# Fused convolution block and window-attention block: the order of a strip, the second MLP bias, and who subtracts the softmax maxima

## The reference, cut to what matters

```python
x = relu(bn3(conv1x1(relu(bn2(conv3x3_grouped(relu(bn1(conv1x1(x)))))))) + x)
shortcut = x
y = roll(layernorm(x, norm1_w, norm1_b), (-3, -3))      # then cut in 7x7 windows
q, k, v = y @ qkv_w.T
attn = softmax(q @ k.T * 0.25 + bias(cpb MLP) + mask)
x = shortcut + unroll((attn @ v) @ proj_w.T + proj_b)
z = layernorm(x, norm2_w, norm2_b)
return x + gelu(z @ fc1_w.T + fc1_b) @ fc2_w.T + fc2_b
```

## Time and profile before

| | |
|---|---|
| median of 3 runs | 4876.97 us (4873.29 to 4880.41) |
| the profiled execution, its own time | 4880.38 us |
| span of that execution in the profile | 4878.6 us |
| busy over the span: PE, DVE, ACT, POOL | 94%, 75%, 73%, 52% |
| granted TensorE clock, mean over the span | 0.99 of full speed |
| convolution stage | its last sums on DVE end about 754 us after the span's start |
| attention stage | the remaining 4120 us or so, 256 strips |

### The profile page before, as it was taken

One profiled execution on the slowest core, in us unless ns is written; L12 is line 12 of the kernel. 1 busy time (PEld: TensorE's weight loads), 2 busy tenths in 40 slices (PEclk: granted clock), 3 DMA queues, 4 the chain that ended last, 5 costly groups with the idle time before them and its releaser, 6 DMA issues.

```text
span 4878.6 us, 192818 instructions
## 1 busy us (share of the span) xinstructions
PE 4590.0 (94%) x71190; PEld 3230.5 (66%) x71190; DVE 3646.7 (75%) x7461; ACT 3537.4 (73%) x5899; POOL 2552.6 (52%) x3498
## 2 busy tenths in 40 slices
PE   8999996999999999999999999999999999999998
PEld 5666664666666666666666666666666666666665
DVE  4343435888888888888888888888888888888886
ACT  3344444778778777877877877877787787787786
POOL 4344433555555555555555555555555555555554
PEclk9999998999999999999999999999999999999999
DMA  4445441100000100100100000010010010000000
GB/s 134 153 145 158 144 136 39 28 26 27 26 26 26 28 26 26 28 27 26 28 27 26 27 28 27 26 28 26 26 28 27 26 28 27 27 27 26 26 26 24
DMA packets 298299, 218.70 MB, mean 45 GB/s; under 512 B 43247, under 2 KB 245486, under 8 KB 298158
## 3 DMA queue, kind: packets, MB, share of 16 engines
q1 hardware_dynamic: 294632, 215.41, 15.1%
q10 hardware_dynamic: 3526, 1.12, 0.1%
HBM read 110.78 MB, written 111.94 MB: 46 GB/s over the span
## 4 chain that ended last, share of the span: by engine, by line
PE 64%; DVE 19%; issue 11%; ACT 5%; DVEq 1%; POOL 0%; DMA 0%; ACTq 0%; POOLq 0%
DVE xn L1084 9%; PE bank L577 8%; PE bank L658 7%; PE bank L633 6%; PE bank L502 6%; PE bank L569 5%; DVE sc L1059 5%; PE bank L600 5%; PE bank L515 4%; PE bank L649 4%; PE bank L560 3%; PE bank L587 3%; DVE z L1084 3%; ACT L862 2%; PE bank L480 2%
## 5 line engine op out<-in xcount | busy, mean ns | idle before, releaser
L1084 DVE SCALAR_TENSOR_TENSOR xn<-x,lnp 98x128 f32<-98x128 f32 x1024 | 874.0, 912 | 3.7 <-POOL lnp L1154 3.7
L1218 POOL TENSOR_TENSOR res<-x,projb 98x512 f32<-98x512 f32 x256 | 325.8, 1273 | 1013.9 <-DVE x L1101 1013.9
L1236 POOL TENSOR_TENSOR sc<-sc,mx 128x784 f32<-128x784 f32 x512 | 788.6, 1540 | 57.2 <-DVE mx L1065 57.2
L658 PE MATMUL bank<-g,fc_sb 128*128 128x392 f32 x2048 | 784.6, 506 | 0.2
L1059 DVE TENSOR_TENSOR sc<-bank,shared 128x392 f32<-128x392 f32 x1024 | 529.7, 560 | 310.5 <-PE bank L587 310.5
L862 ACT ACTIVATE g<-bank,fc1b 128x392 f32<-128x392 f32 x1024 | 574.1, 586 | 125.8 <-PE bank L651 112.5
L649 PE MATMUL bank<-zt_hi,fc_hi 128*128 128x392 f32 x1024 | 453.8, 443 | 153.1 <-ACT g L862 147.7
L600 PE MATMUL bank<-ident_sb,sc 128*113 128x128 f32 x4096 | 530.9, 273 | 0.3 <-ACT shared L872 0.2
L1154 POOL TENSOR_TENSOR lnp<-st 98x8 f32<-98x8 f32 x777 | 145.8, 216 | 731.6 <-DVE st L927 728.0
L600 PEld LDWEIGHTS bank<-ident_sb,sc 128*113 128x113 f32 x4096 | 515.6, 177 | 3.0 <-ACT shared L872 0.7
L1065 DVE TENSOR_REDUCE mx<-sc 128x16 f32<-128x784 f32 x512 | 496.7, 970 | 18.4
(11 more groups left out here) (106 smaller groups left out, 9187.0 us busy)
## 6 DMA issues: line engine op xcount, KB each, us to landing
x<-x_scratch SPq DMA_DIRECT2D x768, 49.0 KB
out_x<-y SPq DMA_DIRECT2D x672, 49.0 KB
xc_even<-in_x SPq DMA_DIRECT2D x128, 196.0 KB
shared<-in_x SPq DMA_DIRECT2D x128, 196.0 KB
x_scratch<-xc_even SPq DMA_DIRECT2D x128, 196.0 KB
x_scratch<-shared SPq DMA_DIRECT2D x128, 196.0 KB
x<-x_scratch SPq DMA_DIRECT2D x256, 38.5 KB
out_x<-y SPq DMA_DIRECT2D x224, 38.5 KB
```

Source lines behind the costliest of these rows:

```text
L658: mm = nc.tensor.matmul(RC[:, 0:ST], fc2[:, c, :], g[:, c], start=c == 0, stop=c == HC - 1)
L1084: ins = V.scalar_tensor_tensor(dst[:, p, :], src[:, p, :], lnp[:, 7, i, p:p + 1], lnp[:, 8, i, p:p + 1].to_broadcast([PT, C]), ALU.add, AL ...
L1236: P.tensor_tensor(out=s_r, in0=s_r, in1=m_r.to_broadcast([128, 2 * HEADS, N]), op=ALU.subtract).then_inc(sub_done, 1)
```

## The change

1. **Order.** PE transposes z first, projects k before q, does both halves of the values together, transposes probabilities 0 and 1 ahead of the hidden layers, and runs hidden 0 and 1, both score halves, hidden 2 and 3, both `mlp_out` and both `attend` without anything between their halves. On ACT the gelu table is loaded in advance and the four gelus stand together; `yt_out` moves ahead of `reciprocals`. On DVE `x1_norm` moves from behind the second `maxima` to before the first `biased`; the statistics of x1 move from the front of step t-1 to behind the softmax's part of step t-2 (`x1_stats(beyond)`).
2. **q_out** moves from ACT to DVE.
3. **subtract** moves from POOL to DVE, each half right behind its `maxima`.
4. **The second MLP bias** is added in ACT's copy `yt_out` (bias by channel); `residual2` and its buffer go away, x2 gets two buffers, and `y_sum` adds x2.
5. **POOL** keeps `residual1` (now of strip t, at the front of the step) and then `factors`.
6. The loop begins one strip earlier (strips 4 and 5 are its first two).

```diff
 def over_strips(e, body):
-    for c in range(-1, 5):
+    for c in range(-1, 4):
         body(Strip(0, c))
     with e.Fori(0, (NS - 6) // 2) as k:
+        body(Strip(k, 4))
         body(Strip(k, 5))
-        body(Strip(k, 6))
-    for c in range(NS - 1, NS + 3):
+    for c in range(NS - 2, NS + 3):
@@ ACT
             def yt_out(t):
-                nc.scalar.activation(yt[:], RC[:, 0:ST], ACT.Copy).then_inc(c_out, 1)
+                nc.scalar.activation(yt[:], RC[:, 0:ST], ACT.Identity, bias=fc2b[:]).then_inc(c_out, 1)
@@ DVE
+            def q_out(t):
+                dve.wait_ge(a_full, A_JOBS * t.n + 3)
+                wait(dve, s_full, t.n)
+                V.tensor_copy(qt[:, :, 0:N], RA[:, 0:ST].rearrange("c (w n) -> c w n", n=N)).then_inc(a_out, 1)
+            def subtract(t, r):
+                dve.wait_ge(max_done, 2 * t.n + r + 1)
...
+                V.tensor_tensor(out=s_r, in0=s_r, in1=m_r.to_broadcast([128, 2 * HEADS, N]),
+                                op=ALU.subtract).then_inc(sub_done, 1)
...
                 if t.there():
                     v_out(t)
+                    q_out(t)
+                if t.fixed and t.c == -1:
+                    x1_stats(ahead)
                 if ahead.there():
-                    x1_stats(ahead)
+                    x1_norm(ahead)
...
                 if t.there():
                     biased(t, 0)
                     maxima(t, 0)
+                    subtract(t, 0)
                     biased(t, 1)
                     maxima(t, 1)
-                if ahead.there():
-                    x1_norm(ahead)
+                    subtract(t, 1)
+                if beyond.there():
+                    x1_stats(beyond)
                 if t2.there():
                     x2_norm(t2)
@@ POOL
             def strips(t):
-                ahead, t1, t2 = t.back(-1), t.back(1), t.back(2)
+                ahead, t2 = t.back(-1), t.back(2)
+                if t.there():
+                    residual1(t)
                 if ahead.there() or t2.there():
                     factors(t)
-                if t.there():
-                    subtract(t)
-                if t2.there():
-                    residual2(t2)
-                if ahead.there():
-                    residual1(ahead)
```

More of the change, by code:

```diff
@@ L574, in project @@
             def project(t, i):
+                part = 1 - i
                 wait(pe, a_out, A_JOBS * t.n + 1 + i)
-                nc.tensor.matmul(RA[:, 0:ST], wqkv[:, C * i:C * i + C], xt[:],
+                nc.tensor.matmul(RA[:, 0:ST], wqkv[:, C * part:C * part + C], xt[:],
                                  start=True, stop=True).then_inc(a_full, 1)
@@ L677, in strips @@
                 if t.there():
+                    project(t, 0)
                     values(t, 0)
+                    values(t, 1)
                     project(t, 1)
[L680 to L690, removed]
                 if t1.there():
@@ L694, in strips @@
                 if t3.there():
+                    hidden(t3, 0)
+                    hidden(t3, 1)
+                if t.there():
+                    scores(t, 0)
+                    scores(t, 1)
+                if t3.there():
+                    hidden(t3, 2)
                     hidden(t3, 3)
@@ L751, in _ @@
             load(projb[:], everywhere("proj_b", PT))
-            load(fc2b[:], everywhere("fc2_b", PT))
+            load(fc2b[:], column("fc2_b"))
             for i, nm in enumerate(("norm1_w", "norm1_b", "norm2_w", "norm2_b")):
@@ L833, in xt_out @@
                                      bias=ln[:, 1:2]).then_inc(a_out, 1)
[L835 to L839, removed]
             def v_out(t):
@@ L847, in k_out @@
             def k_out(t):
-                act.wait_ge(a_full, A_JOBS * t.n + 3)
+                act.wait_ge(a_full, A_JOBS * t.n + 2)
+                wait(act, s_full, t.n)
                 for hh in range(2):
@@ L912, in strips @@
                     exponentials(t, 0)
+                if t3.there():
+                    yt_out(t3)
                 if t1.there():
                     reciprocals(t1)
-                if t3.there():
-                    yt_out(t3)
                 if ahead.there():
@@ L1093, in x2_norm @@
                 wait(dve, c_full, C_JOBS * (t.n - 1) + 1)
-                norm(1, t.n + 3, x2, z, z_sb)
+                norm(1, t.n + 3, x2[:, t.u], z, z_sb)
             def x2_out(t):
@@ L1098, in x2_out @@
                 dve.wait_ge(res1_sb, t.n + 1)
-                wait(dve, res2_sb, t.n)
-                wait(dve, z_sb, t.n)
-                V.tensor_tensor(out=x2[:].rearrange("p k c -> p (k c)"), in0=RB[1][0:PT, :],
+                wait(dve, z_sb, t.n - 1)
+                wait(dve, c_out, C_JOBS * (t.n - 1))
+                V.tensor_tensor(out=x2[:, t.u].rearrange("p k c -> p (k c)"), in0=RB[1][0:PT, :],
                                 in1=res1[:, t.u].rearrange("p k c -> p (k c)"), op=ALU.add).then_inc(b_out[1], 1)
@@ L1109, in y_sum @@
                 wait(dve, y_out[t.u], 16 * MOVES * t.half)
-                dve.wait_ge(res2_sb, t.n + 1)
                 V.tensor_tensor(out=y[:, t.u].rearrange("p k c -> p (k c)"), in0=RC[0:PT, :],
-                                in1=res2[:, t.u].rearrange("p k c -> p (k c)"), op=ALU.add).then_inc(c_out, 1)
+                                in1=x2[:, t.u].rearrange("p k c -> p (k c)"), op=ALU.add).then_inc(c_out, 1)
             def strips(t):
-                ahead, t1, t2, t3 = t.back(-1), t.back(1), t.back(2), t.back(3)
+                beyond, ahead, t1, t2, t3 = t.back(-2), t.back(-1), t.back(1), t.back(2), t.back(3)
                 if t3.there():
```

41 lines of the change are left out of this document (11 added, 30 removed).

## The result

The changed kernel takes 5151.85 us (median of 4 runs, 5144.96 to 5157.38) against 4875.83 (4873.29 to 4880.41) for the kernel before: a ratio of 1.0564, with an interval of 1.0546 to 1.0583. That is 276 us slower. The prediction said slower, 5060 us with a range of 4950 to 5150: the sign is right, the size is short by 92 us, and the range misses the median by 2 us. The profiled execution is the one of 5144.96, with a span of 5142.8 us.

What follows compares the result with a forecast made beforehand. Bound: a closed ring of waits through PE and DVE, one turn per strip, which the change lengthens through POOL. Sum: 4880.4 + 120 (POOL ring) + 62 (late loads) = 5062, said as 5060 us; range 4950 to 5150.

Steps and rivals of the forecast that it cites:

- But POOL now closes a longer ring: `x1_norm` on DVE waits for POOL's factors, behind `residual1`: a strip takes 16.34 us, 0.47 over 15.87; times 256, +120 us.
- DVE's half of the ring: Scores to next projection: `x1_norm`'s 3.34 us out, two 0.97 us subtractions and 0.79 of statistics in; 8.70 us against 9.25.
- Faster: Rival: the subtraction on DVE takes 0.49 us instead of 0.97, the ring is 15.38 us, 4847 us in all; chance 0.04.
- Dearer: Rival: the DVE subtraction costs 1.06 us (+46) or PE's clock falls at wraps (+38): above 5110 us, chance 0.14.
- Loads that come late: Where rows wrap, DVE's earlier statistics of x1 wait about 2.0 us for a load: 31 strips, +62 us.
- PE's half: Projection start to scores end on PE: eight transposes add 0.87 us, quicker hidden 0 and 1 save 0.38; 7.22 against 6.73.
- Quicker: Rival: POOL's factors take some tenths less and loads land 1 us earlier: 4963 us, class 4895 to 5000, chance 0.15.
- No change: Rival: POOL's ring and the loads have unseen slack, the ring through the scores holds at 15.92 us: 4880 to 4895, chance 0.05.
- the clock: PE's idle time before projections might lower its clock: 1.2 x 31 = +38 us at wraps, left out of the sum.

Runs made afterwards that it cites:

- Run 6: The changed kernel with both subtractions moved back from DVE to POOL, behind the factors, all else as changed: 4837.17 us, 0.9924 of the kernel before.
- run 1: Also `fill`: the changed kernel plus six spare matmuls on PE ahead of each projection, their result overwritten: 5045.17 us, 1.0345 of the kernel before.
- run 2: Also `stats_late`: the changed kernel with the statistics of x1 moved from ahead of `x2_norm` to behind `y_sum`: 4769.05 us, 0.9785 of the kernel before.
- run 8: Also `late_res1_dve`: run 2's kernel with `residual1` moved from POOL to DVE, behind `q_out`: 4823.39 us, 0.9891 of the kernel before.
- run 7: Also `late_sub_pool`: run 2's kernel with both subtractions moved back from DVE to POOL, behind the factors: 4633.45 us, 0.9502 of the kernel before.
- run 3: The changed kernel with `residual1` placed behind the factors on POOL instead of in front: 5261.26 us, 1.0795 of the kernel before.
- run 4: The changed kernel with both the statistics of x1 behind `y_sum` and `residual1` behind the factors on POOL: 4994.38 us, 1.0243 of the kernel before.
- run 5: The kernel before with only the two subtractions moved from POOL to DVE, each behind its maxima: 4817.86 us, 0.9883 of the kernel before.

## Why the prediction was right and wrong

- **But POOL now closes a longer ring**: right. The norm starts 6.81 after the projection (3014.78 to 3021.59; the prediction had 7.89 - 1.05 = 6.84), the wait before it is 1.97 ("about 2 us"), an undisturbed strip is 16.28 (predicted 16.34). Against 15.85 that is 110 us, where the sum had 120. That 6.81 and 6.84 agree so closely is partly luck: from the projection to `x2_out` the prediction had 1.14 and the strip shows 1.34 (3014.78 to 3016.12), and for the factors it had 3.65, from the start-up strip, where the strip shows 3.46 (3018.13 to 3021.59). The two errors cancel.
- **DVE's half of the ring**: right. The subtraction takes 977 ns (0.97 taken), the norm 347 (338 taken). "Faster", which needed 0.54, is out, as is the 1.06 of "Dearer". The trace agrees with the estimate of 0.974 us by the Trainium skill, "VectorE: DVE Perf Modes", section on the errata.
- **Loads that come late**: right. 31 strips are longer by 2.0, 63 us (62 in the sum). The statement that an ordinary strip's load is just in time holds too: 28.3 us in 15 waits, all at wraps, is all there is in the 2000 us. Run 6, in which DVE asks for the load some 1.8 us sooner, shows how near it was, with 111 waits.
- **PE's half**: right. The scores end 7.23 after the start of the projection (3020.95 + 1.06 - 3014.78; predicted 7.22), and the first `biased` starts at 7.86, behind the norm. "Quicker" and "No change" asked for a wait before the norm that is short or absent; it is the longest regular one on DVE.
- **The step that failed is the clock**: "a gap inside dense work it doesn't show, so I leave it out of the sum and in the range". In the range it stood as 1.2 x 31 = +38, at the wrap strips alone. The count by strips gives 116, and run 1, which takes most of it away, 107 with what else it changes. Behind a wrap the loss is 50 us, 1.7 for each strip, not far from the 38. The larger part, 66 us, lies where I had none: in strips without any late load, whose gap before the projection is only 1.8 to 1.9 us. Behind about half of such gaps the clock falls, and each fall costs 1.0.

Two errors lie in this. I took the gaps of the earlier trace rows, 3.5 us with 1.17 us of work, as the nearest row and concluded about gaps of that length alone, though the change puts a gap into every one of 256 strips. And for the wrap strips I took 3.3 us at the lower level from the same row. Behind 10 wraps that is about what it was, and the strip lost 1.0 (1.2 predicted); behind 20 the clock stayed down for 5.3 to 6.8 us, and the strip lost 2.0. The slack of PE's half, 0.42, was priced well enough: between the end of the scores and `biased` there are 0.63 us in the strip shown, less the 0.25 that DVE takes to start.

The Trainium skill, "TensorE: Matmul & The Clock Gate", section "Why this matters for your kernels", advises against idle gaps between bursts of matmuls from a certain length on. By its figure only the gaps at the wraps (3.93 us at 3132.84) would pay, as in "Dearer"; the trace shows the clock fall behind a gap of 1.87 us (3097.18), so for this kernel the figure is too generous, and 66 us of the result lie between the two.

With the measured terms (110 for the ring, 63 for the loads, 116 for the clock) the sum is 4876 + 110 + 63 + 116 - 19 = 5146, against 5151.85. The 19 us of the start-up the prediction had not looked for.

## What to carry to other kernels

When a change opens an idle gap on TensorE in each turn of a loop, price the clock for each turn, not just for the longest gaps (here a gap of 1.1 us in each turn, run 2, or of 1.3, run 8, cost nothing, and one of 1.8 to 1.9 cost 1.0 us about every second time); `fill` is a cheap way to find out what it is worth, and moving DVE work out of the ring so that the gap closes is the better cure. A term put in the range because no row shows it should be bounded by how often it could happen, which here was in each of 256 strips and not in 31. Whether an operation belongs on DVE or POOL is decided by the place and not by the engine's speed: the same subtraction on DVE gained 58 us in the old order and lost 315 in the new one.

## What the runs showed of the hardware

DVE and POOL hold each other up when both read two operands from SBUF, and it can be either of them that pays:

| on DVE | on POOL beside it | held up | alone | together |
|---|---|---|---|---|
| norm 98x128 | subtraction 128x784 | DVE | 338 ns | 659 (run 7) |
| norm 98x128 | subtraction 128x784, then sum 98x512 | DVE | 338 ns | 912 (before) |
| norm 98x128 | sum 98x512 | DVE | 347 | 595 (runs 3, 4) |
| subtraction 128x784 | sum 98x512 | POOL | 1.27 us | 1.82 (run 5) |
| sum 98x512 | power 98x8 | POOL | 1.65 us | 2.13 (run 8) |

The 659, 912 and 595 are means over the norm's four instructions, of which one or two are held up and the others take their 0.34. In the kernel before, the windows cut so that the instructions come apart show the first that is held:

```profile
3022.63 1.56 POOL L1236 TENSOR_TENSOR sc<-sc,mx 128x784 f32<-128x784 f32 x1 [0.25 <-DVE mx L1065]
```

```profile
3022.73 1.61 DVE L1084 SCALAR_TENSOR_TENSOR xn<-x,lnp 98x128 f32<-98x128 f32 x1
```

The next one starts at 3024.26, behind POOL's other sum at 3024.15, and takes 1.36; so the 3.42 of the earlier trace rows are a wait for the second subtraction and one for `residual2`. In every row the one that started first kept its time: POOL at 3018.49 before DVE at 3018.55 in run 3, DVE at 3012.02 before POOL at 3012.24 in run 5, DVE at 3007.34 before POOL's power at 3007.38 in run 8.

The Trainium skill, "SBUF — State Buffer", section "Who interferes with whom", describes this: a DVE instruction with two SBUF inputs and a GpSimd instruction that reads SBUF exclude each other, and the one that issues first has the ports. The trace agrees in all five rows. What I had not expected is that `residual1` and the factors, already short, are worth placing with this in mind: it went with a loss of 109 us against the changed kernel in run 3, and with one of 225 us against `stats_late` in run 4, some 46 of them by the clock.

The clock's falls lie behind the longer gaps in every trace. Leaving out each kernel's start-up and its end, none of the ten traces has one behind a gap before the projection of less than 1.67 us; `stats_late` (1.1) and `late_res1_dve` (1.3) have none at all.

What stays open: why the clock falls behind a gap of 1.8 to 1.9 us in some strips and not in others (the gap before 3031.08 was 1.86, and that strip lost no time). And whether `late_sub_pool` could gain the 1.27 of its second norm by setting `ot_out` ahead of it; that was not tried.
